# Edge pass of a two-layer graph network: first statistics in the middle of the step, for the group two back; norm rows one step later; a projection between the spreads; powers first on GpSimd

## The chip, the cores and the metric

The kernel runs on one core of one Trainium2 chip, as one program. The metric is the time of the device in microseconds. The kernel before has a median of 2852.71 us over 3 runs (2852.1 to 2857.18).

## The reference, cut to what matters

```
h = maximum(layernorm(x), 0)                       # x: [50000, 128] f32
x = x + HGT(h, node_type (3), edges (25000), edge_type (4))
h = maximum(layernorm(x), 0)
x = x + GraphConv(relu, W2)(GraphConv(relu, W1)(h))

HGT: k, q, v = per-type projections of h; per edge, 8 heads:
  att   = (q[dst] * (k[src] @ rel_att[type])).sum(-1) * rel_pri / sqrt(16)
  alpha = softmax of att over the edges of one dst
  aggr  = segment_sum(alpha * (v[src] @ rel_msg[type]), dst)
  trans = gelu(aggr) @ Wa[type] + ba[type]
  res   = trans * sigmoid(skip) + h * (1 - sigmoid(skip))
  out   = layernorm(res) * ln_g[type] + ln_b[type]
```

The edges are sorted by destination, so a segment sum is a scan along the edges that is reset where the destination changes.

## The kernel before, in words

The kernel runs in phases with barriers between them: tables of the nodes, an attention phase, a softmax over segments (`soft_`), the edge pass (`edge_`, lines 1215 to 1560 of the program), and two graph convolutions (`conv1`, `conv2`). The change lies in the edge pass, beside one allocation at the head.

The edge pass takes 196 tiles of 128 edge places in 28 groups of G = 7 tiles, and each group in two parts (`CK`): 4 tiles (512 columns) and 3 tiles (384). Each engine has a program of its own, written out by hand as a loop over steps s, and semaphores are the only order between them. In before there are 28+3 steps. What a group goes through, with the line of each operation:

- **Spread** (TensorE, L1440, L1443): the softmax weight and the carry factor of each edge are spread over the head's rows into PSUM (`wB`, `dB`), one buffer each.
- **Gather** (VectorE, `gathered`): `msg_all` times `wB` (L1499), then the scan with `dB` (L1503), which carries on from the last column of the part before.
- **Gelu** (ScalarE, L1395) into `gl`, and the **mask product** (GpSimd, L1368), which multiplies `gl` by a mask per node type, `glm`.
- **Projection** (TensorE, `project`): an identity matmul that adds the residual input `hb` (L1453), a bias matmul per tile (L1455), and three matmuls per tile for the types (L1459), all into `pc`, two buffers.
- **First statistics** (VectorE, `spreads(0, ..)`, L1510, L1514, L1518): mean and variance of the projection, plus epsilon. **First power** (GpSimd, L1386): to the power of -1/2. **Scale term** (VectorE, L1528). **Normalisation** (ScalarE, L1407) into `x1`.
- **Gains** (TensorE, L1468, `pg`, one buffer): gain and bias of the layernorm per edge. VectorE multiplies (L1547), adds (L1549), and adds the residual row `xr` (L1551).
- **Second statistics** (VectorE, `spreads(1, ..)`, the same lines), **second power** (GpSimd, L1380), **norm-row terms** (L1535, L1538), **norm rows** (ScalarE, L1420), the store to the table (SyncE, L1344). The residual rows are stored at L1350.
- SyncE loads rows (L1323), one-hot rows (L1327) and masks (L1334) one step ahead. ScalarE prepares `hb` from the rows (L1428).

In step s of before VectorE does: gather(s, first part); scale term(s-2); norm-row terms(s-3); gather(s, second part); gains and residual of s-2, both parts; second statistics(s-2); first statistics(s-1). TensorE: spread(s, 0); gains(s-2, 0); spread(s, 1); project(s-1, 0); gains(s-2, 1); project(s-1, 1). GpSimd: both mask products of s; second power(s-2); first power(s-1). ScalarE: gelu(s, 0); normalisation(s-2); gelu(s, 1); norm rows(s-3); `hb`(s). The names `edge_x`, `edge_sc` and `edge_st` in the profile are `x1`, `sc3` and `st`; `reset` in the profile of this phase is `dhat`.

Of the kernel before, what the change touches and what calls it, by code (L numbers as in the profile page):

```python
# [5 lines left out]
F32 = mybir.dt.float32  # L6
# [7 lines left out]
P = 128  # L14
D = 128
# [48 lines left out]
def hgt_then_graphconv(nc, x, src, dst, edge_type, node_type, Wk, bk, Wq, bq, Wv, bv, Wa, ba, rel_pri, rel_att,  # L64
                       rel_msg, skip, ln_g, ln_b, W1, b1, W2, b2, out):
    top = ExitStack()
    with top, nc.allow_non_contiguous_dma(reason="small parameter and index lists"):
# [55 lines left out]
        rel_k = sb("rel_k", [P, RELS, D], F32)  # L123
        rel_v = sb("rel_v", [P, RELS, D], F32)
# [1148 lines left out]
        with ExitStack() as ctx:  # L1273
# [6 lines left out]
            two, three, four = range(2), range(3), range(4)  # L1280
            xr = [lb(f"xr{b}", [P, G, NW], F32) for b in four]
            mask = [lb(f"mask{k}", [P, 4, TYPES, P], BF16) for k in two]
            oh = [lb(f"oh{b}", [K9, GC], BF16) for b in three]
# [4 lines left out]
            hs = lb("hs", [P, G, D], F32)  # L1288
# [11 lines left out]
            xr_in = [ls(f"xr_in{b}") for b in four]  # L1300
            mask_in = [ls(f"mask_in{b}") for b in two]
            oh_in = [ls(f"oh_in{b}") for b in three]
# [6 lines left out]
            st_done, var1, var2, rstd1, rstd2 = ls("st_done"), ls("var1"), ls("var2"), ls("rstd1"), ls("rstd2")  # L1309
# [7 lines left out]
            with nc.Block() as block:  # L1317
                @block.sync
                def _(sp):
                    def load(g):  # L1320
                        if g >= 4:
                            sp.wait_ge(nm2, g - 3)
                        sp.dma_start(xr[g % 4][:], xd_rows[g * GC:(g + 1) * GC].rearrange("(t p) w -> p t w", p=P)).then_inc(xr_in[g % 4], 16)  # L1323
                        if g >= 3:
                            sp.wait_ge(pg_ready, (g - 2) * 2)
                        for k in range(SPLIT):
                            sp.dma_start(oh[g % 3][k:K9:SPLIT].rearrange("t (n e) -> t n e", e=P),  # L1327
                                         type_row[g * G:(g + 1) * G, TYPES:2 * TYPES].rearrange("n t e -> t n e")).then_inc(oh_in[g % 3], 16)
# [9 lines left out]
                    for s in steps:  # L1338
                        if on(s + 1):
                            load(s + 1)  # L1340
                        g = s - 3
                        if on(g):
                            sp.wait_ge(hs_done, g + 1)
                            sp.dma_start(ta[g * GC:(g + 1) * GC].rearrange("(t p) d -> p t d", p=P), hs[:]).then_inc(hs_out, 16)  # L1344
                        if on(s + 1):
                            load_masks(s + 1)
                        g = s - 2
                        if on(g):
                            sp.wait_ge(x1_done, g + 1)
                            sp.dma_start(x1_rows[g * GC:(g + 1) * GC].rearrange("(t p) d -> p t d", p=P), x1[g % 3][:]).then_inc(x1_out[g % 3], 16)  # L1350
# [5 lines left out]
                def _(pool):  # L1356
# [14 lines left out]
                    for s in steps:  # L1371
                        if on(s):
                            masked(s, 0)
                            masked(s, 1)
                        if on(s - 2):
                            b = (s - 2) % 2
                            pool.wait_ge(var2, s - 1)
                            if s >= 4:
                                pool.wait_ge(nm2, s - 3)
                            pool.tensor_tensor(rstd[1][b][:], ve[1][b][:], mh[:], ALU.pow).then_inc(rstd2, 1)  # L1380
                        if on(s - 1):
                            b = (s - 1) % 2
                            pool.wait_ge(var1, s)
                            if s >= 3:
                                pool.wait_ge(y_done, s - 2)
                            pool.tensor_tensor(rstd[0][b][:], ve[0][b][:], mh[:], ALU.pow).then_inc(rstd1, 1)  # L1386

                @block.scalar
                def _(act):
# [7 lines left out]
                    for s in steps:  # L1397
                        if on(s):
                            gelu(s, 0)
                        g = s - 2  # L1400
# [11 lines left out]
                        if on(s):  # L1412
                            gelu(s, 1)
                        g = s - 3
                        if on(g):
                            act.wait_ge(nm2, g + 1)
                            if g >= 1:
                                act.wait_ge(hs_out, g * 16)
                            for j in range(G):
                                m = nc.scalar.activation(hs[:, j], x1[g % 3][:, j], ACT.Relu, bias=nmr[1][g % 2][:, j:j + 1],  # L1420
                                                         scale=sc3[g % 2][:, j:j + 1])
                            m.then_inc(hs_done, 1)
                        if on(s):
                            act.wait_ge(xr_in[s % 4], s // 4 * 16 + 16)
                            if s >= 2:
                                act.wait_ge(pc_ready, (s - 1) * 2)
                            for j in range(G):
                                nc.scalar.activation(hb[s % 2][:, j], xr[s % 4][:, j, 0:D], ACT.Relu, bias=xr[s % 4][:, j, C_NA:C_NA + 1],  # L1428
                                                     scale=xr[s % 4][:, j, C_RA:C_RA + 1]).then_inc(hb_done, 1)

                @block.tensor
                def _(pe):
# [12 lines left out]
                    def project(g, ck):  # L1445
                        j0, j1 = CK[ck]
                        if ck == 0:
                            pe.wait_ge(oh_in[g % 3], g // 3 * 48 + 48)
# [279 lines left out]
```

## Time and profile before

| | before |
|---|---|
| median of 3 runs | 2852.71 us |
| the profiled execution, device time | 2854.7 us |
| its span, first to last instruction | 2853.0 us |
| mean granted clock of TensorE, whole span | 0.777 |
| busy share: TensorE, VectorE, ScalarE, GpSimd | 65%, 72%, 41%, 58% |
| edge pass, first load to last store issued | 1585.7 to 2077.9 us |

The profile comes from one execution of the program, recorded by the hardware. Times are in us from the start of the span. In a row of the order of time the columns are: start, duration, engine, line, operation, output<-inputs, shapes, count; in brackets the idle time of the engine before it and who ended it. PE is TensorE, PEld its weight loads, DVE VectorE, ACT ScalarE, POOL GpSimd, SP SyncE. PEclk is the granted clock, 1.00 for 2.4 GHz and 0.50 for 1.2 GHz. Where several instructions of one line are merged into one row, the duration is that of them all.

### The profile page before, as it was taken

The numbers are of one execution on the slowest core, as the hardware profiler recorded it, in microseconds if no ns is written. First come the engines' busy times: TensorE is split into PE (matmuls) and PEld (weight loads), VectorE is DVE, ScalarE is ACT, GpSimd is POOL, SyncE is SP. The second block draws the span as 40 slices with busy tenths as digits, with TensorE's granted clock in tenths as the row PEclk, the third lists the DMA queues.
The fourth block names the chain that finished last, engine by engine and source line by source line (L and its number), as shares of the span: only waits on it lengthen the run. The fifth ranks groups of instructions, "written<-read, shape, count | busy, mean of one in ns | idle before, by whom it ended". The sixth has DMA issues, their size and how long they took to land. (4 is left out here: it accounts for less than half of the span.)

```text
span 2853.0 us, 48869 instructions
## 1 busy us (share of the span) xinstructions
PE 1866.8 (65%) x12706; PEld 1449.3 (51%) x12706; DVE 2062.4 (72%) x7060; ACT 1159.7 (41%) x3211; POOL 1655.0 (58%) x1737
## 2 busy tenths in 40 slices
PE   4630001999999999999992677887757763333332
PEld 1100000999999999999992344444435442222221
DVE  7994563999999999999996777777745553333333
ACT  0000001777777777777771345554422221111111
POOL 0002334777777777777761354455467767777776
PEclk9985555999999999999996798899855555555555
DMA  2006774777777777776761344444344442222222
GB/s 52 0 0 202 249 247 134 172 185 184 183 183 184 181 184 185 185 181 184 182 171 33 91 127 123 122 118 124 102 122 132 131 118 72 71 71 70 71 70 52
DMA packets 400270, 374.38 MB, mean 131 GB/s; under 512 B 60254, under 2 KB 342269, under 8 KB 397032
## 3 DMA queue, kind: packets, MB, share of 16 engines
q1 hardware_dynamic: 360856, 276.76, 35.3%
q0 software_dynamic: 31360, 64.76, 10.7%
q10 hardware_dynamic: 7806, 29.98, 2.6%
q8 instruction: 104, 1.70, 0.2%
q14 instruction: 144, 1.18, 0.2%
HBM read 227.43 MB, written 147.13 MB: 131 GB/s over the span
## 5 line engine op out<-in xcount | busy, mean ns | idle before, releaser
L1683 DVE TENSOR_TENSOR_SCAN conv_sT<-keep,conv_sT,conv_pT 128x128 f32<-128x128 bf16 x390 | 187.1, 480 | 384.3 <-PE conv_pT L1658 383.5
L1658 PE MATMUL conv_pT<-ident,conv_row 128*128 128x128 f32 x392 | 182.1, 464 | 405.2 <-ACT conv_row L1643 328.3
L814 POOL DMA_INDIRECT att_xsd<-xt,ends_i x392 | 390.2, 995 | 95.1 <-issue 94.7
L1658 PEld LDWEIGHTS conv_pT<-ident,conv_row 128*128 128x128 f32 x392 | 74.5, 190 | 496.2 <-ACT conv_row L1643 384.9
L995 PE MATMUL att_kvc<-att_hm,w_kv 128*128 128x128 f32 x2352 | 295.9, 276 | 0.0
L939 ACT ACTIVATE att_nhb<-att_nxr 128x128 f32<-128x128 f32 x391 | 168.8, 478 | 276.6 <-DMA att_nxr<-xt 276.6
L995 PEld LDWEIGHTS att_kvc<-att_hm,w_kv 128*128 128x128 f32 x2352 | 279.6, 193 | 0.0
L1368 POOL TENSOR_TENSOR edge_glm<-edge_gl,edge_mask 128x1536 f32<-128x1536 f32 (+1 forms) x56 | 153.1, 2735 | 214.2 <-PE edge_pc L1459 207.4
L1664 PE MATMUL conv_pm<-w,conv_sT 128*128 128x128 f32 x784 | 258.9, 434 | 12.1 <-DVE conv_res L1690 11.0
L1643 ACT ACTIVATE conv_row<-conv_row,ats 128x128 f32<-128x128 f32 x196 | 78.6, 401 | 425.3 <-DMA conv_row<-t,idx 425.3
L1108 DVE TENSOR_TENSOR att_kvm<-att_kvc,att_rel_in 128x1024 f32<-128x1024 f32 x196 | 240.0, 1224 | 13.1 <-PE att_kvc L1008 1.2
L1008 PE MATMUL att_kvc<-tab,att_noh 9*128 9x128 bf16 x391 | 53.4, 216 | 279.7 <-DMA att_noh<-node_hot 276.7
L1606 POOL DMA_INDIRECT conv_row<-t,idx x196 | 192.0, 979 | 69.4 <-issue 38.4
L1612 POOL DMA_INDIRECT out_dram<-conv_res,out_i x196 | 197.3, 1006 | 59.7 <-issue 58.5
L1606 POOL DMA_INDIRECT conv_row<-ta,idx x196 | 185.1, 944 | 68.2 <-issue 52.4
L1664 PEld LDWEIGHTS conv_pm<-w,conv_sT 128*128 128x128 f32 x784 | 205.9, 323 | 32.5 <-DVE conv_sT L1683 29.0
L1044 PE MATMUL att_keyp<-att_kvm,rel_k 128*128 128x128 f32 x1568 | 207.4, 275 | 0.5 <-DVE att_prod L1140 0.5
L1046 PE MATMUL att_msgp<-att_kvm,rel_v 128*128 128x128 f32 x1568 | 207.1, 275 | 0.0
L1044 PEld LDWEIGHTS att_keyp<-att_kvm,rel_k 128*128 128x128 f32 x1568 | 190.5, 192 | 4.4 <-issue 0.9
L1046 PEld LDWEIGHTS att_msgp<-att_kvm,rel_v 128*128 128x128 f32 x1568 | 190.8, 192 | 0.0
L829 POOL TENSOR_TENSOR att_not<-att_nx,rb_all 128x256 f32<-128x256 f32 x196 | 142.5, 727 | 82.1 <-DMA out_dram<-att_not 50.9
L1151 DVE TENSOR_TENSOR att_hm<-att_hT,att_mask_in_t 128x768 f32<-128x768 f32 x196 | 186.2, 950 | 3.2 <-DMA att_mask_in_t<-type_row 3.2
(240 smaller groups left out, 4883.6 us busy)
## 6 DMA issues: line engine op xcount, KB each, us to landing
att_mask_in_t<-type_row SPq DMA_DIRECT2D x196, 192.0 KB
xt<-xr ACTq DMA_DIRECT2D x23, 1224.0 KB
att_nxr<-xt SPq DMA_DIRECT2D x97, 262.0 KB
att_rel_in<-rel_row SPq DMA_DIRECT2D x196, 128.0 KB, 3.2
out_dram<-att_not SPq DMA_DIRECT2D x97, 256.0 KB, 3.8
ta<-att_nhs SPq DMA_DIRECT2D x97, 256.0 KB
xr<-in_x_dram SPq DMA_DIRECT2D x22, 1088.0 KB
xd_rows<-att_xsd SPq DMA_DIRECT2D x196, 65.5 KB, 3.1
```

What stands on the lines that cost most here:

```text
L814: pool.indirect_dma_start(out=xsd[:, v, k, :], out_offset=None, in_=xt, in_offset=bass.IndirectOffsetOnAxis(ap=ends_i[:, n, k:k + 1], axis ...
L939: m = nc.scalar.activation(nhb[:, u % 2, i], nxr[g % RN][:, j, 0:D], ACT.Relu, bias=nxr[g % RN][:, j, C_NA:C_NA + 1], scale=nxr[g % RN][:, ...
L995: nc.tensor.matmul(kvc[:, e], w_kv[:, t, e], hm[:, w, 0, t], start=e == 0 and t == 0, stop=False)
L1044: nc.tensor.matmul(keyp[:, 0], rel_k[:, r], kvm[:, w, 0, r], start=r == 0, stop=r == RELS - 1)
L1046: m = nc.tensor.matmul(msgp[:, 0], rel_v[:, r], kvm[:, w, 1, r], start=r == 0, stop=r == RELS - 1)
L1108: dve.tensor_tensor(kvm[:, w], kvc[:, 0:2].rearrange("p a (o e) -> p a o e", o=1).to_broadcast([P, 2, RELS, P]), rel_in[:, v].rearrange("p ...
L1151: dve.tensor_tensor(hm[:, w], hT[:, 0:2].rearrange("p e (o d) -> p e o d", o=1).to_broadcast([P, 2, TYPES, P]), mask_in_t[:, k % RM], ALU. ...
L1606: pool.indirect_dma_start(out=row[:, n % R, :], out_offset=None, in_=table, in_offset=bass.IndirectOffsetOnAxis(ap=idx[:, int(second), n:n ...
L1612: pool.indirect_dma_start(out=out, out_offset=bass.IndirectOffsetOnAxis(ap=out_i[:, k:k + 1], axis=0), in_=res[:, k % R, :], in_offset=Non ...
L1658: nc.tensor.transpose(pT[:, n % 2, 0:P], row[:, n % R], ident[:]).then_inc(t_ready, 1)
L1664: nc.tensor.matmul(pm[:, k % 2, 0:D], sT[:, k % R], w[:], start=True, stop=True).then_inc(m_ready, 1)
L1683: dve.tensor_tensor_scan(sT[:, n % R], keep[:, n * P:(n + 1) * P], pT[:, n % 2, 0:P], before, ALU.mult, ALU.add).then_inc(s_ready, 1)
```

## The change

VectorE's step becomes: gains and residual (s-3, first part); gather(s, first part); norm-row terms(s-4); first statistics(s-2); gains(s-3, second part); gather(s, second part); scale term(s-2); residual(s-3, second part); second statistics(s-3). TensorE: spread(s, 0); gains(s-3, 1); project(s-1, 0); spread(s, 1); project(s-1, 1); gains(s-2, 0). GpSimd: first power(s-2), both mask products of s, second power(s-3). ScalarE: `hb`(s); gelu(s, 0); norm rows(s-4); gelu(s, 1); normalisation(s-2). There are 28+4 steps. The rows get a fifth buffer, the one-hot rows a fourth, and `hs` takes the place of the relation tables, which are no longer read in this phase. The semaphore of the statistics is split in two.

```diff
-        rel_k = sb("rel_k", [P, RELS, D], F32)
-        rel_v = sb("rel_v", [P, RELS, D], F32)
+        rel_kv = sb("rel_kv", [P, 2, RELS, D], F32)
+        rel_k, rel_v = rel_kv[:, 0], rel_kv[:, 1]
...
-            hs = lb("hs", [P, G, D], F32)
+            hs = rel_kv[:].rearrange("p a r d -> p (a r) d")[:, 0:G]
-            steps = range(groups + 3)
+            steps = range(groups + 4)
 # sync
+                        if g >= 5:
+                            sp.wait_ge(nm2, g - 4)
+                        sp.dma_start(xr[g % 5][:], ...
                         if g >= 4:
-                            sp.wait_ge(nm2, g - 3)
-                        sp.dma_start(xr[g % 4][:], ...
-                        if g >= 3:
-                            sp.wait_ge(pg_ready, (g - 2) * 2)
+                            sp.wait_ge(pg_ready, (g - 3) * 2)
...
                         g = s - 3
                         if on(g):
+                            sp.wait_ge(x1_done, g + 1)
+                            sp.dma_start(x1_rows[...], x1[g % 3][:]).then_inc(x1_out[g % 3], 16)
+                        if on(s + 1):
+                            load_masks(s + 1)
+                        g = s - 4
+                        if on(g):
                             sp.wait_ge(hs_done, g + 1)
                             sp.dma_start(ta[...], hs[:]).then_inc(hs_out, 16)
-                        if on(s + 1):
-                            load_masks(s + 1)
-                        g = s - 2
-                        if on(g):
-                            sp.wait_ge(x1_done, g + 1)
-                            sp.dma_start(x1_rows[...], x1[g % 3][:]).then_inc(x1_out[g % 3], 16)
 # gpsimd
+                        g = s - 2
+                        if on(g):
+                            b = g % 2
+                            pool.wait_ge(var1, g + 1)
+                            if g >= 2:
+                                pool.wait_ge(y_done, g - 1)
+                            pool.tensor_tensor(rstd[0][b][:], ve[0][b][:], mh[:], ALU.pow).then_inc(rstd1, 1)
                         if on(s):
                             masked(s, 0)
                             masked(s, 1)
-                        if on(s - 2):            # second power, then first power(s - 1)
...
+                        g = s - 3                # second power
...
 # scalar: hb(s), gelu(s, 0), norm rows (s - 4), gelu(s, 1), normalisation (s - 2)
 # tensor
                         if on(s):
                             spread(s, 0)
-                        if on(s - 2):
-                            gains(s - 2, 0)
+                        if on(s - 3):
+                            gains(s - 3, 1)
+                        if on(s - 1):
+                            project(s - 1, 0)
                         if on(s):
                             spread(s, 1)
                         if on(s - 1):
-                            project(s - 1, 0)
+                            project(s - 1, 1)
                         if on(s - 2):
-                            gains(s - 2, 1)
-                        if on(s - 1):
-                            project(s - 1, 1)
+                            gains(s - 2, 0)
 # vector
+                    def gained(g, ck):           # multiply and add, as before
...
+                    def residual(g, ck):
+                        js = slice(*CK[ck])
+                        dve.wait_ge(pg_read, g * 2 + ck + 1)
+                        m = dve.tensor_tensor(x1[g % 3][:, js], x1[g % 3][:, js], xr[g % 5][:, js, 0:D], ALU.add)
+                        if ck:
+                            m.then_inc(x1_done, 1)
                     for s in steps:
+                        g = s - 3
+                        if on(g):
+                            gained(g, 0)
+                            residual(g, 0)
                         if on(s):
                             gathered(s, 0)
+                        g = s - 4                # norm-row terms, wait for rstd2
...
+                        g = s - 2
+                        if on(g):
+                            spreads(0, g, pc[g % 2], var1)
+                        g = s - 3
+                        if on(g):
+                            gained(g, 1)
+                        if on(s):
+                            gathered(s, 1)
                         g = s - 2
                         if on(g):
                             dve.wait_ge(rstd1, g + 1)
                             dve.scalar_tensor_tensor(nmr[0][g % 2][:], ...).then_inc(nm1, 1)
                         g = s - 3
                         if on(g):
+                            residual(g, 1)
                             dve.wait_ge(x1_done, g + 1)
-                            stats[0] += 1
-                            spreads(1, g, x1[g % 3], stats[0], var2)
-                        g = s - 1
-                        if on(g):
-                            stats[0] += 1
-                            spreads(0, g, pc[g % 2], stats[0], var1)
+                            spreads(1, g, x1[g % 3], var2)
```

## Rows read from the trace of the kernel before

**Rows 1.** The windows view: busy time of each engine in 100 us of the pass.
```profile
core 0: us, PE busy (x) PEld busy (x) DVE busy (x) ACT busy (x) POOL busy (x), PEclk, DMA share, GB/s
1800.00:1900.00 100.00, 78.60 (x407) 47.61 (x405) 78.81 (x256) 50.69 (x133) 50.55 (x24) 0.91 0.44 124
```

**Rows 2.** Order of time: VectorE's first gather product, fourth and last full step.
```profile
1624.42 0.69 DVE L1499 TENSOR_TENSOR msg_all<-edge_wB,msg_all 128x512 f32<-128x512 f32 x1
...
2034.40 0.69 DVE L1499 TENSOR_TENSOR msg_all<-edge_wB,msg_all 128x512 f32<-128x512 f32 x1
```

**Rows 3.** Order of time: one steady step, VectorE, TensorE and GpSimd.
```profile
1915.66 1.28 DVE L1503 TENSOR_TENSOR_SCAN msg_all<-edge_dB,msg_all 128x512 f32<-128x512 f32 x1
...
1918.43 1.92 PE L1453 MATMUL edge_pc<-edge_hb,ident 128*128 128x512 f32 x2
...
1918.75 1.02 DVE L1503 TENSOR_TENSOR_SCAN msg_all<-edge_dB,msg_all 128x384 f32<-128x384 f32 x1 [1.00 <-PE edge_dB L1443]
1919.68 0.66 DVE L1547 TENSOR_TENSOR edge_x<-edge_x,edge_pg 128x512 f32<-128x512 f32 x1
...
1920.63 2.94 PE L1459 MATMUL edge_pc<-w_a,edge_glm 128*128 128x128 f32 x24
...
1923.75 3.10 POOL L1368 TENSOR_TENSOR edge_glm<-edge_gl,edge_mask 128x1536 f32<-128x1536 f32 x1 [7.17 <-PE edge_pc L1459]
...
1924.11 0.56 DVE L1547 TENSOR_TENSOR edge_x<-edge_x,edge_pg 128x384 f32<-128x384 f32 x1 [2.32 <-PE edge_pg L1468]
...
1925.05 2.27 PE L1459 MATMUL edge_pc<-w_a,edge_glm 128*128 128x128 f32 x18
1925.29 1.98 DVE L1551 TENSOR_TENSOR edge_x<-edge_x,edge_xr 128x384 f32<-128x384 f32 x1
...
1927.49 2.37 POOL L1368 TENSOR_TENSOR edge_glm<-edge_gl,edge_mask 128x1152 f32<-128x1152 f32 x1 [0.64 <-PE edge_pc L1459]
...
1928.02 1.02 PE L1443 MATMUL edge_dB<-reset,expand 112*128 112x512 f32 x2
...
1929.40 0.49 DVE L1518 TENSOR_SCALAR edge_ve<-edge_mv 128x7 f32<-128x7 f32 x1
1929.80 1.47 DVE L1510 BATCH_NORM_STATS2 edge_st<-edge_pc 128x6 f32<-128x128 f32 x7
...
1931.92 0.17 DVE L1518 TENSOR_SCALAR edge_ve<-edge_mv 128x7 f32<-128x7 f32 x1
```

**Rows 4.** Order of time, end of the pass: residual addition alone; the last norm rows.
```profile
2058.13 0.56 DVE L1551 TENSOR_TENSOR edge_x<-edge_x,edge_xr 128x384 f32<-128x384 f32 x1
...
2075.03 2.80 ACT L1420 ACTIVATE edge_hs<-edge_x,edge_nmr,edge_sc 128x128 f32<-128x128 f32 x7 [4.74 <-DVE edge_nmr L1538]
```

**Rows 5.** Order of time, attention phase: VectorE with two SBUF operands beside GpSimd.
```profile
1193.77 0.72 POOL L829 TENSOR_TENSOR att_not<-att_nx,rb_all 128x256 f32<-128x256 f32 x1 [1.61 <-DMA out_dram<-att_not]
1193.81 0.70 DVE L1090 SCALAR_TENSOR_TENSOR att_nnm<-att_nmv,att_nrs 128x4 f32<-128x4 f32 x1
...
516.71 1.25 DVE L1090 SCALAR_TENSOR_TENSOR att_nnm<-att_nmv,att_nrs 128x4 f32<-128x4 f32 x1
517.05 0.19 POOL L821 COPY ats<-att_xsd 128x6 f32<-128x6 f32 x1
517.21 0.72 POOL L829 TENSOR_TENSOR att_not<-att_nx,rb_all 128x256 f32<-128x256 f32 x1
```

**Rows 6.** Order of time, attention phase: a sum of two SBUF operands during a power.
```profile
492.34 1.68 POOL L848 TENSOR_TENSOR att_nrs<-att_nve,att_mh 128x8 f32<-128x8 f32 x1
...
493.06 0.42 DVE L1143 TENSOR_TENSOR att_nx<-att_nx,att_nxr 128x256 f32<-128x256 f32 x1
```

**Rows 7.** Order of time, start of the pass: the very first projection, at full clock.
```profile
1597.57 1.02 PE L1453 MATMUL edge_pc<-edge_hb,ident 128*128 128x512 f32 x2
...
1598.85 2.94 PE L1459 MATMUL edge_pc<-w_a,edge_glm 128*128 128x128 f32 x24
```

**Rows 8.** The windows view of TensorE alone: a steady step, and early in the pass.
```profile
1918.60:1920.40 1.80, 1.80 (x5) 0.51 0.87 240
...
1610.60:1612.40 1.80, 1.80 (x3) 0.50 0.90 268
```

More of the change, by code:

```diff
@@ L1279, in hgt_then_graphconv @@
             CK = ((0, 4), (4, G))
-            two, three, four = range(2), range(3), range(4)
-            xr = [lb(f"xr{b}", [P, G, NW], F32) for b in four]
+            two, three, four, five = range(2), range(3), range(4), range(5)
+            xr = [lb(f"xr{b}", [P, G, NW], F32) for b in five]
             mask = [lb(f"mask{k}", [P, 4, TYPES, P], BF16) for k in two]
-            oh = [lb(f"oh{b}", [K9, GC], BF16) for b in three]
+            oh = [lb(f"oh{b}", [K9, GC], BF16) for b in four]
             gl = lb("gl", [P, GC], F32)
@@ L1299, in hgt_then_graphconv @@
             pg = lp("pg", [P, 4, GW], F32)
-            xr_in = [ls(f"xr_in{b}") for b in four]
+            xr_in = [ls(f"xr_in{b}") for b in five]
             mask_in = [ls(f"mask_in{b}") for b in two]
-            oh_in = [ls(f"oh_in{b}") for b in three]
+            oh_in = [ls(f"oh_in{b}") for b in four]
             x1_out = [ls(f"x1_out{b}") for b in three]
@@ L1398, in _ @@
                         if on(s):
-                            gelu(s, 0)
+                            act.wait_ge(xr_in[s % 5], s // 5 * 16 + 16)
+                            if s >= 2:
+                                act.wait_ge(pc_ready, (s - 1) * 2)
+                            for j in range(G):
+                                nc.scalar.activation(hb[s % 2][:, j], xr[s % 5][:, j, 0:D], ACT.Relu, bias=xr[s % 5][:, j, C_NA:C_NA + 1],
+                                                     scale=xr[s % 5][:, j, C_RA:C_RA + 1]).then_inc(hb_done, 1)
+                            gelu(s, 0)
+                        g = s - 4
+                        if on(g):
+                            act.wait_ge(nm2, g + 1)
+                            if g >= 1:
+                                act.wait_ge(hs_out, g * 16)
+                            for j in range(G):
+                                m = nc.scalar.activation(hs[:, j], x1[g % 3][:, j], ACT.Relu, bias=nmr[1][g % 2][:, j:j + 1],
+                                                         scale=sc3[g % 2][:, j:j + 1])
+                            m.then_inc(hs_done, 1)
+                        if on(s):
+                            gelu(s, 1)
                         g = s - 2
@@ L1467, in gains @@
                         for j in range(j0, j1):
-                            m = nc.tensor.matmul(pg[:, j - j0], oh[g % 3][:, j * P:(j + 1) * P], tab9[:, CW:CW + GW], start=True, stop=True)
+                            m = nc.tensor.matmul(pg[:, j - j0], oh[g % 4][:, j * P:(j + 1) * P], tab9[:, CW:CW + GW], start=True, stop=True)
                         m.then_inc(pg_ready, 1)
@@ L1504, in gathered, with spreads @@
                                                ALU.mult, ALU.add).then_inc(scan_done, 1)
-                    def spreads(k, g, of, done, then):
+                    def spreads(k, g, of, then):
+                        measured = st1_done if k else st0_done
                         for j in range(G):
@@ L1510, in spreads @@
                             m = dve.bn_stats(st[:, k, j], of[:, j])
[L1511 to L1512 removed]
+                        m.then_inc(measured, 1)
+                        dve.wait_ge(measured, g + 1)
                         for j in range(G):
```

93 lines of the change are left out of this document (32 added, 61 removed).

## The prediction

> **What bounds the kernel now.** I read the page first, then the windows of the edge pass, then one step of it in order of time, because shares of a span cannot say which wait ends last. In the windows VectorE and TensorE are each busy 79% of the stretch and GpSimd half [rows 1]: nobody is full, so the step is a loop of waits. It repeats exactly: 24 periods from 1624.42 to 2034.40 are 17.08 us each [rows 2].
>
> The loop [rows 3]: the first scan ends at 1916.94. TensorE then does the second spread and the first projection of the group before, to 1920.63+2.94 = 1923.57. Only then can GpSimd's first mask product start (1923.75 to 1926.85), and only then the gain matmuls for which VectorE had waited 2.32 us. VectorE's last residual addition starts at 1925.29 and takes 1.98 us, where the same one takes 0.56 us with GpSimd idle [rows 4]; it ends just after the mask product. The second projection ends at 1925.05+2.27 = 1927.32, the second mask product runs from 1927.49 to 1929.86, and the 7-element addition of epsilon that falls into it takes 0.49 us instead of 0.17 and ends with it. The first statistics (1929.80 to 1932.09) and the next step follow. VectorE so loses 1.0 (second scan) + 2.3 (gains) + 1.4 (residual) + 0.3 (epsilon) = 5.0 us a step; 12.1 us is its work.
>
> **What blocks VectorE beside GpSimd.** This decides the forecast. An operation of VectorE with two SBUF operands stands still while a GpSimd product runs: one of 4 elements, 0.15 us alone, took 0.70 us from 1193.81, beside a product that ended at 1194.49 [rows 5]. At 516.71 one took 1.25 us, through two GpSimd operations that stood back to back [rows 5], so the seam between two such does not let VectorE in. A product with a PSUM operand is not touched (0.56 us at 1924.11, inside the first mask product) [rows 3]. The power is another thing: a sum of two SBUF operands took its usual 0.42 us in the middle of one [rows 6], so a power blocks nothing.
> The Trainium skill (SBUF — State Buffer, Who interferes with whom) says that a VectorE instruction with two SBUF inputs contends with any GpSimd instruction that reads SBUF. The power reads SBUF, and the row speaks against the rule there. By the page the first residual addition would wait about 0.15 us a step for the second power, 4 us in all; by the row nothing.
>
> **The change, part by part.** One new steady step on VectorE, 0 being the start of its first gain product, durations from [rows 3] unless said:
> - Gains and residual of the first four tiles of the group three back: three operations of 0.7 us, to 2.1. Their inputs come from the step before. The wait of 2.3 us goes here.
> - Gather, first part: product 0.7, scan 1.28, to 4.05. Two small norm-row operations, to 4.35; the power they need came at the end of the step before.
> - First statistics: 1.47+0.6+0.17, to 6.55. Their projection is a step old and GpSimd is idle, so nothing blocks.
> - Gains of the last three tiles: two operations of 0.56, to 7.7. Gather, second part: product to 8.2, then scan 1.02 once its spread is there, to 9.3.
> - GpSimd: the first power stands ahead of the masks, 6.6 to 8.1 (1.48, an estimate from the 1.68 of 8 elements [rows 6]); then the first mask product, 8.1 to 11.2.
> - VectorE's scale term and last residual addition both read two SBUF operands. They come up at 9.3 and are blocked until 11.2: a new stall of 1.9 us in place of the old ones.
> - Second statistics: 2.1, with an epsilon at their end that the second mask product can block.
>
> TensorE with the clock at 2.4 GHz: gain matmuls at 1.4, after the second gain operation, the identity matmul some 0.4 later; from identity to the end of the 24 matmuls took 1598.85+2.94-1597.57 = 4.2 us [rows 7], so the first projection ends at 6.1. The spread of 512 took 1927.32 to 1929.04, 1.7 us; that of 384, at three quarters, 1.3, ends at 7.4. Second projection 3.4, to 10.8. The next gains and spread end at 13.2. The second scan finds its spread ready: TensorE leaves VectorE's loop, and the wait of 1.0 goes.
>
> The second mask product (2.37 us) needs that projection plus 0.17, and so it decides the period:
> *Long step.* Ready at 11.0, it stands behind the first (end 11.2) without a seam, to 13.6, and VectorE is let in only then: scale term 0.15, residual 0.56, statistics 2.1. Period 16.4.
> *Short step.* With the projection 0.3 us or more late VectorE slips in at 11.2; scale term and residual are done at 11.9, aggregation at 14.0, and the epsilon ends with the second product. With a lateness x the period is 10.8+x+0.17+2.37+0.17 = 13.5+x, and not under about 14.3.
> The clock sets x. Now it is at 1.2 GHz for part of each step after 3.2 us of idle, and early in the pass it was so after 1.4 us of idle too [rows 8]; the identity then takes 1.92 us [rows 3] instead of 1.02 [rows 7]. In a long step TensorE idles from 13.2 to 17.8, in a short one some 2 us. So I expect a slow stretch in most steps: gain matmuls +0.3 and rest +0.2 (estimates), identity +0.9, x = 1.4, period 14.9. With one long step in four, (3x14.9+16.4)/4 = 15.3, which I take. Ends for a steady step: 14.4 and 16.5.
>
> Covered, at nothing: ScalarE has 50.7 us of work in 100 [rows 1], 8.7 a step; its normalisation starts after the scale term at 11.4, is half done by 12.9 and done by 14.0, before VectorE's next step wants it. Late by a us there would be a us per step. SyncE: the input load waits for the norm terms at 4.35 and is wanted by ScalarE some 10 us later; the masks stand behind the store of the residual rows, issued at 12, and are wanted at 8.1 of the next step, 11 us later; the table store goes out near 15 and its buffer is wanted 5 us later. DMA is 44% busy [rows 1], and no wait in [rows 3] is for a transfer. The powers stay two. The fifth input buffer, fourth one-hot buffer and shared place of the norm rows issue nothing.
>
> Start and end. From [rows 7] the very first projection ends at 1601.8; then spread 1.5, projection 3.4, spread 1.8, projection 4.3, spread 1.5, projection 3.4, gains 0.6: the fourth step starts at 1618.3 and its gather at 1620.4, against 1624.4 now [rows 2], 4 us earlier. The last full step starts 24 periods on. From there: one period; 10.3 for a step that TensorE's last projections bound; 8.9 and 6.2 for two of VectorE alone; 4.8 for power, terms and norm rows. The end is at 1618.3+25P+30.2 = 1648.5+25P, with P = 15.3 at 2031.0. Now it is 2075.03+2.80 = 2077.8 [rows 4]: 46.8 us gained. The added step of the tail is in this: from the last full step's gather the rest takes 43.4 us now and 43.5 then.
>
> The profiled execution took 2854.7 us (span 2853.0, 1.7 around it), 2.0 over the median 2852.7. 2854.7-46.8 = 2807.9, in terms of the median 2806.
>
> **Rivals.**
> 1. *Long steps throughout.* P = 16.4: end 2058.5, gain 19, time 2833. For it: the back-to-back rows, and a margin of 0.2 us only. Against: TensorE would idle 4.6 us in such a step, and 3.2 already brings the low clock. Chance 0.19.
> 2. *Hardly any block.* The scale term finds a way in, or less is locked than I read: VectorE's 12.1 and TensorE's 12 us decide, P = 13, gain 104, time 2748; half-way (14.2) 2778. For it: powers block nothing. Against: the 1.98 us row and the two of [rows 5]. Chance 0.10.
> 3. *Slower: the low clock takes hold of the projection.* P passes 17.07 when the second projection is 3.6 us late, which needs 7.2 of its 9.4 us at 1.2 GHz. At 17.8 the time is 2868, with all of it slow (P about 20) 2924. For it: the low clock comes after short idles too. Against: TensorE would be busy from 1.4 to 13.2 with no wait. Chance 0.06.
> 4. *It does not do what it says:* masks, queued behind the residual store, or input rows arrive late and take 1.7 us a step back. P = 17.0, 2848. For it: shorter leads. Against: DMA at 44%. Chance 0.05.
> The forecast has 0.60, with 2788 to 2821 (P 14.6 to 15.9) by itself.
>
> **How the numbers follow.** A measurement here tells about 0.2%, 6 us, from nothing. Faster: forecast, rivals 1 and 2, 0.89, of which I keep 0.87. Within: most of rival 4, 0.05. Slower: rival 3 and what could ride on it, 0.08. The range goes from P = 14.4 (gain 69) to a little past the long step: 2783 to 2839.
>
> **What would show it.** Right: steps of 15 to 16 us; a scale term of about 2 us that ends with the first mask product; no wait of the last gain product or second scan for TensorE; first statistics while GpSimd idles; the last epsilon ending with the second mask product. Wrong: scale terms of 0.14 us (rival 2), of 4 us in every step (rival 1), a granted clock under 0.8 in the pass (rival 3), GpSimd or ScalarE waiting for a DMA (rival 4).

## The result and the profile after

The changed kernel takes 2786.8 us (median of 4 runs, 2786.3 to 2789.5). Its ratio to the kernel before is 0.977, with a 95% interval of 0.975 to 0.978: 66 us less. (One of the four executions of the kernel before took 3608 us and is left out.) The forecast was 2806 in a range of 2783 to 2839, so the direction and the range hold, but the gain is two fifths larger than the 47 us worked out.

| | before | after |
|---|---|---|
| span of the profiled execution | 2853.0 | 2784.7 us |
| start of the last norm rows | 2075.0 | 2005.8 us |
| mean of the 24 steady periods | 17.08 | 14.375 us |

All of it came from the edge pass: the last norm rows end 69.2 us earlier. The page, first section (engine, busy time and its share of the span, instructions): the same instructions as before.
```profile
PE 1840.5 (66%) x12706; PEld 1453.7 (52%) x12706; DVE 2059.3 (74%) x7060; ACT 1168.4 (42%) x3211; POOL 1660.8 (60%) x1737
```
The windows of the pass, in the columns of [rows 1], which answers to it. VectorE is busy 92 of 100 us instead of 79. The granted clock is the same in this stretch; over the 24 steady periods it is 0.94, against 0.90 before.
```profile
1800.00:1900.00 100.00, 86.64 (x462) 57.64 (x461) 91.83 (x300) 63.78 (x161) 59.22 (x29) 0.91 0.56 147
...
1616.50:1961.50 345.00, 300.38 (x1635) 198.59 (x1633) 321.14 (x1030) 218.36 (x549) 206.35 (x96) 0.94 0.54 143
```
The steps are not alike. Measured from one first gain product of VectorE to the next, 14 of the 24 are 13.6 to 13.9 us long, seven 14.65 to 14.74 and three 16.1 to 16.3. Here are rows of a short one in order of time; it starts at 1630.10 and the next at 1643.94. It answers to [rows 3].
```profile
1636.45 0.17 DVE L1520 TENSOR_SCALAR edge_ve<-edge_mv 128x7 f32<-128x7 f32 x1
1636.70 1.48 POOL L1378 TENSOR_TENSOR edge_rstd<-edge_ve,edge_mh 128x7 f32<-128x7 f32 x1 [4.95 <-DVE edge_ve L1520]
1638.15 5.81 POOL L1368 TENSOR_TENSOR edge_glm<-edge_gl,edge_mask 128x1536 f32<-128x1536 f32 x2
1638.46 2.27 PE L1460 MATMUL edge_pc<-w_a,edge_glm 128*128 128x128 f32 x18
1639.11 2.16 DVE L1567 SCALAR_TENSOR_TENSOR edge_nmr<-edge_mv,edge_rstd 128x7 f32<-128x7 f32 x1
1641.19 0.54 DVE L1534 TENSOR_TENSOR edge_x<-edge_x,edge_xr 128x384 f32<-128x384 f32 x1
1641.77 1.45 DVE L1512 BATCH_NORM_STATS2 edge_st<-edge_x 128x6 f32<-128x128 f32 x7
1643.86 0.17 DVE L1520 TENSOR_SCALAR edge_ve<-edge_mv 128x7 f32<-128x7 f32 x1
1643.94 0.69 DVE L1527 TENSOR_TENSOR edge_x<-edge_x,edge_pg 128x512 f32<-128x512 f32 x1
```
Two things are to be seen. The scale term of 7 elements takes 2.16 us and ends with the first mask product: this is the stall the forecast put there. And the residual addition behind it, which reads two SBUF operands, runs at 1641.19 although the two mask products stand back to back (one row of 5.81 us, where 3.10+2.37 is 5.47). VectorE was let in at the seam (the moment between the two products), and GpSimd waited for it. With the view cut at the seam, another such step shows the second product at 2.77 us against its usual 2.37, beside the same addition.
```profile
1627.34 0.54 DVE L1534 TENSOR_TENSOR edge_x<-edge_x,edge_xr 128x384 f32<-128x384 f32 x1
...
1627.35 2.77 POOL L1368 TENSOR_TENSOR edge_glm<-edge_gl,edge_mask 128x1152 f32<-128x1152 f32 x1
```
A step of 16.2 us, in order of time, starts at 1875.23 and ends at 1891.46:
```profile
1879.98 4.58 PE L1460 MATMUL edge_pc<-w_a,edge_glm 128*128 128x128 f32 x24
...
1885.25 0.56 DVE L1500 TENSOR_TENSOR msg_all<-edge_wB,msg_all 128x384 f32<-128x384 f32 x1 [2.44 <-PE edge_wB L1441]
...
1886.70 2.27 PE L1460 MATMUL edge_pc<-w_a,edge_glm 128*128 128x128 f32 x18
1886.89 0.96 DVE L1567 SCALAR_TENSOR_TENSOR edge_nmr<-edge_mv,edge_rstd 128x7 f32<-128x7 f32 x1
1889.15 2.37 POOL L1368 TENSOR_TENSOR edge_glm<-edge_gl,edge_mask 128x1152 f32<-128x1152 f32 x1 [1.31 <-PE edge_pc L1460]
1890.46 1.08 DVE L1520 TENSOR_SCALAR edge_ve<-edge_mv 128x7 f32<-128x7 f32 x1
1891.46 0.67 DVE L1527 TENSOR_TENSOR edge_x<-edge_x,edge_pg 128x512 f32<-128x512 f32 x1
```
Here the first projection's 24 matmuls take 4.58 instead of 2.94 us, the second projection ends late, at 1888.97, the second mask product starts behind it at 1889.15, and the epsilon is held until it ends at 1891.52. There is a new wait too: the second gather product stands 2.44 us for its spread, which the change put behind the first projection. The windows of TensorE over a step of 13.86, one of 16.29 and one of 14.66 us (columns: stretch, length, TensorE busy, granted clock, DMA share, GB/s) show what parts them:
```profile
1643.94:1657.80 13.86, 11.62 (x68) 1.00 0.60 154
1701.03:1717.32 16.29, 14.79 (x68) 0.79 0.53 142
1717.32:1731.98 14.66, 13.19 (x68) 0.88 0.51 140
```

### The profile page after: what moved, and what is told of

Its sections match the earlier page's. It is cut to its first block and busy times, and to the rows that moved or that the text cites. A ratio compares the mean times of both kernels' runs of the same rounds, so it can differ in the third digit from the quotient of the medians.

```text
span 2784.7 us, 48869 instructions
## 1 busy us (share of the span) xinstructions
PE 1840.5 (66%) x12706; PEld 1453.7 (52%) x12706; DVE 2059.3 (74%) x7060; ACT 1168.4 (42%) x3211; POOL 1660.8 (60%) x1737
## 5 line engine op out<-in xcount | busy, mean ns | idle before, releaser
L1044 PE MATMUL att_keyp<-att_kvm,rel_kv 128*128 128x128 f32 x1568 | 207.4, 275 | 0.5 <-DVE att_prod L1140 0.5
L1046 PE MATMUL att_msgp<-att_kvm,rel_kv 128*128 128x128 f32 x1568 | 207.1, 275 | 0.0
L1044 PEld LDWEIGHTS att_keyp<-att_kvm,rel_kv 128*128 128x128 f32 x1568 | 190.5, 192 | 4.4 <-issue 0.9
L1046 PEld LDWEIGHTS att_msgp<-att_kvm,rel_kv 128*128 128x128 f32 x1568 | 190.8, 192 | 0.0
L1063 DVE BATCH_NORM_STATS2 att_nst<-att_nx 128x6 f32<-128x128 f32 x782 | 186.3, 279 | 0.2
```

What stands on the lines that cost most here:

```text
L1044: nc.tensor.matmul(keyp[:, 0], rel_k[:, r], kvm[:, w, 0, r], start=r == 0, stop=r == RELS - 1)
L1046: m = nc.tensor.matmul(msgp[:, 0], rel_v[:, r], kvm[:, w, 1, r], start=r == 0, stop=r == RELS - 1)
L1063: m = dve.bn_stats(nst[:, k, i], of[:, u % 2 * 2 + i])
```

## The experiments

They ran in three rounds, each with the kernel before beside it; the changed kernel itself ran beside them only in the second. On the chips of the first and third round that kernel took 2957 and 2970 us, on the second 2851. In the profiles the time behind the edge pass is the longer one there (from the last norm rows to the end 867 us in the first kernel below, 776 in the changed kernel's own profile), while a step at full clock takes the same 13.85 us (two added matmuls, below). So the rounds are compared by ratios and by steps. A step is always measured between VectorE's gain products of 512 columns, and a mean is over the 24 periods from the fourth step on.

**TensorE's order undone.** The second spread goes ahead of the first projection again. The gain matmuls stay where the change put them.
```diff
                             gains(s - 3, 1)
+                        if on(s):
+                            spread(s, 1)
                         if on(s - 1):
                             project(s - 1, 0)
-                        if on(s):
-                            spread(s, 1)
-                        if on(s - 1):
                             project(s - 1, 1)
```


> One part undone: TensorE does the second spread before the first projection again, as in the kernel before; all else as changed. Theory A (the projection must end early enough for GpSimd's second mask product): the second spread waits for the first scan at 4.05 of the step, so the projections end about 1.3 us later; period 14.9 at full clock, 15.6 in the mean against 14.4, so about 2816 us and mask products that start after the projection, not after the power. Rival B (TensorE is off the loop, its order is of no account): 2787 within 6 us.

Ratio 0.9715 (0.9697 to 0.9732), steps of 13.2 to 13.3 and 15 us after a first one of 16.4, mean 13.86. Both theories fell: undoing this part makes the kernel faster than the change as a whole. A step of 13.3 us, in order of time from 1804.57, and the start of the next:
```profile
1813.12 1.02 DVE L1503 TENSOR_TENSOR_SCAN msg_all<-edge_dB,msg_all 128x384 f32<-128x384 f32 x1
1814.06 0.14 DVE L1566 SCALAR_TENSOR_TENSOR edge_nmr<-edge_mv,edge_rstd 128x7 f32<-128x7 f32 x1
1814.11 0.55 DVE L1533 TENSOR_TENSOR edge_x<-edge_x,edge_xr 128x384 f32<-128x384 f32 x1
1814.30 5.66 POOL L1368 TENSOR_TENSOR edge_glm<-edge_gl,edge_mask 128x1536 f32<-128x1536 f32 x2 [1.17 <-PE edge_pc L1460]
1816.80 0.85 DVE L1519 TENSOR_SCALAR edge_ve<-edge_mv 128x7 f32<-128x7 f32 x1
...
1819.34 1.17 DVE L1533 TENSOR_TENSOR edge_x<-edge_x,edge_xr 128x512 f32<-128x512 f32 x1
1819.93 1.92 POOL L1388 TENSOR_TENSOR edge_rstd<-edge_ve,edge_mh 128x7 f32<-128x7 f32 x1
```
The projection is later, as expected, and that holds the first mask product back until 9.7 us into the step, where it began 8.1 us into the one above. By then the scale term (0.14 us) and the residual have gone ahead of it. What is blocked now is the epsilon (0.85 instead of 0.17 us) and 0.5 us of the first residual. The later mask product was a gain here, because it missed VectorE's scale term and last residual.

**Powers last on GpSimd.** The block of the first power is moved behind `masked(s, 1)`.
```diff
+                        if on(s):
+                            masked(s, 0)
+                            masked(s, 1)
                         g = s - 2            # first power
...
-                        if on(s):
-                            masked(s, 0)
-                            masked(s, 1)
```


> One part undone: GpSimd does both mask products first, then the first power (two back), then the second power (three back). Theory A: the first power then waits for the second mask product (ends about 13.4 of the step), VectorE stands at the scale term until 14.9; period about 17.7 against 14.4, 24 x 3.3 = 80 us, about 2867. Rival B (a power of 1.5 us can stand anywhere in an engine that is 60% busy): 2787 to 2800.

Ratio 1.029 (1.028 to 1.031), slower than before, steps of 20.49 us. The mechanism is there: VectorE stands 6.01 us at the scale term for the power that ends behind the second mask product.
```profile
1865.23 2.37 POOL L1368 TENSOR_TENSOR edge_glm<-edge_gl,edge_mask 128x1152 f32<-128x1152 f32 x1 [1.31 <-PE edge_pc L1460]
1867.55 1.48 POOL L1381 TENSOR_TENSOR edge_rstd<-edge_ve,edge_mh 128x7 f32<-128x7 f32 x1
1869.07 0.17 DVE L1567 SCALAR_TENSOR_TENSOR edge_nmr<-edge_mv,edge_rstd 128x7 f32<-128x7 f32 x1 [6.01 <-POOL edge_rstd L1381]
...
1876.66 4.46 PE L1460 MATMUL edge_pc<-w_a,edge_glm 128*128 128x128 f32 x24
```
The step is 2.8 us longer than the 17.7 worked out, because the clock is at 1.2 GHz for part of every step (granted 0.75 over the pass): the 24 projection matmuls take 4.46 instead of 2.94 us and the identity 2.08 instead of 1.02. So the place of the power ahead of the masks carries the change: without it nothing is gained.

**Two more matmuls a step.**
```diff
+                        if ck == 0 and g >= 3:
+                            nc.tensor.matmul(wB[:, 0:w], expand[:, blk], what[:, at:at + w], start=True, stop=True)
+                            nc.tensor.matmul(wB[:, 0:w], expand[:, blk], what[:, at:at + w], start=True, stop=True)
                         nc.tensor.matmul(wB[:, 0:w], ...).then_inc(w_ready, 1)
```


> Two more wB matmuls of 512 columns per step (same operands, same target, before the one that counts), 1.7 us of TensorE, from the fourth step on, where TensorE idles waiting for VectorE. Theory A (steps of 14.7 and 16.2 us are those in which TensorE's clock was at 1.2 GHz after an idle; at full clock a step is 13.85): nearly all steps 13.85, 24 x 0.5 = 12 us less, about 2775, although TensorE does more. Rival B (the long steps come from something else, such as a transfer or the mask products): 2787 or up to 10 us more, steps of 14.7 and 16.2 stay.

Ratio 0.9738 (0.9717 to 0.9760), and every step but the first is 13.84 to 13.86 us, mean 13.88. Theory A holds: with the clock at full (1.00 below, in the columns of [rows 1]) there is no step of 14.7 or 16.2. The gain on the change, 9 us by the ratios, is a little under the 12 expected.
```profile
1800.00:1900.00 100.00, 96.38 (x515) 60.58 (x515) 97.26 (x317) 66.58 (x168) 64.27 (x30) 1.00 0.57 150
```

**Last residual early.** `residual(g, 1)` moves from behind the scale term to right behind `gained(g, 1)`.
```diff
                             gained(g, 1)
+                            residual(g, 1)
...
-                            residual(g, 1)
                             dve.wait_ge(x1_done, g + 1)
```


> The residual addition of the last three tiles moves from behind the scale term to right behind its gains, where GpSimd runs only a power. Theory A (the scale term alone waits for the first mask product, the 0.55 us of the residual behind it is on the path): full-clock steps 13.3 instead of 13.85, low-clock ones as now; 24 x 0.35 = 8 us less, about 2779. Rival B (the addition, which reads two SBUF operands, now holds GpSimd's mask product up by as much): 2787.

Ratio 0.9777 (0.9761 to 0.9793): no gain over the change. The steps run 13.4, 16.3, 14.7 in turn, mean 14.78. The full-clock step is 13.4, as theory A has it, but only a third of the steps are of that kind. In the others the clock was low (granted 0.88 over the pass), and that took the gain back. Rival B is out as well, since the 13.4 is there.

**The changed kernel again,** on the chip of this round.

> The changed kernel as it is, on the chip of the other kernels of this round, so that they can be set against it. Steps of 13.85, 14.7 and 16.2 us, mean 14.4; ratio to the kernel before 0.977.

Ratio 0.977 (0.975 to 0.979), mean step 14.32.

**First statistics behind the second gather.**
```diff
                         g = s - 3
                         if on(g):
                             gained(g, 1)
                         if on(s):
                             gathered(s, 1)
+                        g = s - 2
+                        if on(g):
+                            spreads(0, g, pc[g % 2], var1)
```


> One part moved: the first statistics (two back) stand behind the second gather instead of ahead of the last gains. Theory A (the power, and the mask products queued behind it, wait for these statistics): power to 12.2 of the step, first mask product from 12.2, which catches the scale term: blocked to 15.3, then residual and statistics: steps of 18.2 us, 24 x 3.8 = 91 us more than as changed, slower than before. Rival B (only their being two groups back matters, not the place in the step): steps of 14.4.

Ratio 1.033 (1.031 to 1.034), steps of 20.5 us, slower than before. The sequence is theory A's, power, mask products and then a scale term caught for their first:
```profile
1879.28 1.48 POOL L1378 TENSOR_TENSOR edge_rstd<-edge_ve,edge_mh 128x7 f32<-128x7 f32 x1 [11.59 <-DVE edge_ve L1520]
1880.72 3.09 POOL L1368 TENSOR_TENSOR edge_glm<-edge_gl,edge_mask 128x1536 f32<-128x1536 f32 x1
1880.79 3.05 DVE L1567 SCALAR_TENSOR_TENSOR edge_nmr<-edge_mv,edge_rstd 128x7 f32<-128x7 f32 x1 [1.59 <-POOL edge_rstd L1378]
```
The 2.3 us over the 18.2 expected are again with a clock at 1.2 GHz for part of each step. That the statistics are two groups back is not enough; behind the second gather they hold up the power and the mask products.

**TensorE's order undone, first gather ahead of the first residual.** The edit on TensorE is the one shown above.
```diff
                             gained(g, 0)
-                            residual(g, 0)
                         if on(s):
                             gathered(s, 0)
+                        if on(g):
+                            residual(g, 0)
```


> TensorE's order as before the change (it gave steps of 13.3) and VectorE's first gather ahead of the first residual addition. Theory A (in those steps the loop is: gains, second gather product's spread after the first scan, projection, first mask product, epsilon at the seam): the scan comes 1.0 us earlier, steps of 12.3 to 12.5 at full clock, so 24 us less than with TensorE's order alone, some 36 under the changed kernel. Rival B (VectorE's own work and blocks bound the step, and an order inside it gives nothing): 13.3.

Ratio 0.973 (0.971 to 0.975), mean 14.01. Every second step is 14.33 us, those between are 13.0 to 13.8 with two of 14.6 and 15.1. Wrong for both. In every second step the mask product starts just ahead of the scale term (1761.63 against 1761.99), which then takes 2.77 us; in the next one the scale term is 0.5 us ahead (1776.32 against 1776.86) and takes 0.14. Bringing the chain forward by 1 us brought the mask product into VectorE's way again.
```profile
1761.63 5.82 POOL L1368 TENSOR_TENSOR edge_glm<-edge_gl,edge_mask 128x1536 f32<-128x1536 f32 x2 [0.57 <-PE edge_pc L1460]
1761.99 2.77 DVE L1567 SCALAR_TENSOR_TENSOR edge_nmr<-edge_mv,edge_rstd 128x7 f32<-128x7 f32 x1
...
1776.32 0.14 DVE L1567 SCALAR_TENSOR_TENSOR edge_nmr<-edge_mv,edge_rstd 128x7 f32<-128x7 f32 x1
1776.86 5.50 POOL L1368 TENSOR_TENSOR edge_glm<-edge_gl,edge_mask 128x1536 f32<-128x1536 f32 x2 [1.47 <-PE edge_pc L1460]
```

**The same with epsilon on GpSimd.** The addition of epsilon goes from the end of `spreads` to GpSimd, ahead of each power.
```diff
-                        dve.tensor_scalar_add(ve[k][g % 2][:], mv[k][g % 2][:, :, 1], EPS).then_inc(then, 1)
...
+                            pool.tensor_scalar(ve[0][b][:], mv[0][b][:, :, 1], EPS, None, ALU.add).then_inc(eps_done, 1)
... (the same for the second power, with its wait; TensorE's order and the first gather as above)
```


> As the one with TensorE's order and gather first, and epsilon added by GpSimd ahead of each power instead of by VectorE. Theory A (once the scan is early TensorE's own chain of 12.4 bounds, the block of the epsilon is beside the path): within 0.3 us of the step without this edit, 12.3 to 12.5. Rival B (the epsilon at the seam is what ends the step): a further 0.5 to 1.5 us a step less, 12 to 36 us.

Ratio 0.970 (0.968 to 0.971), median 2764.2 against 2773.5 without the edit on the same chip, so 9 us, less than rival B's least and more than theory A's most. The profiled execution, at 2773.9 us, was ten above the other three (2763.3 to 2764.5), and its mean step of 14.05 can't be set against the 14.01 of the kernel without the edit. What the epsilon is worth alone stays between the two theories.

**The kernel before with more matmuls.**
```diff
+                        if ck == 0 and g >= 3:
+                            for _ in range(3):
+                                nc.tensor.matmul(dB[:, 0:w], expand[:, blk], dhat[:, at:at + w], start=True, stop=True)
                         nc.tensor.matmul(dB[:, 0:w], ...).then_inc(d_ready, 1)
```


> The kernel BEFORE the change, with three more dB matmuls of 512 columns per step (same operands and target, ahead of the one that counts), 2.6 us of TensorE where it idled 3.2 us. Theory A (in the kernel before the 1.2 GHz stretch lies on the loop: second spread +0.8, identity +0.9 us): steps of 15.4 to 15.6 instead of 17.07, 25 x 1.5 = 38 us less, ratio 0.987; so more than half of what the change brought could be had by keeping the clock. Rival B (the added work delays the spread, or the slow stretch is hidden): ratio 1.00 or above.

Ratio 0.996 (0.993 to 0.998), between the two theories. The ten runs fall in two groups, six of 2945 to 2954 us and four of 2967 to 2972, against 2970 for the kernel before. In the profiled one, the slowest of all, the steps go 15.8 and 18.3 in turn, with two of 17.0, mean 17.07. So it settles less than it should. The clock lies on the loop of the kernel before: in the short steps, where it is mostly up (granted 0.94), the wait for the second spread is 0.27 us instead of 1.00 and that for the gains 1.33 instead of 2.32. But these matmuls did not keep it up: it stayed at 0.91, although TensorE was busy 94 of 100 us, and in a long step the 24 matmuls took 4.68 us. Why the clock fell here and not with the two matmuls above is open. An estimate from the steps near full clock: 15.8 in the old order and 13.85 in the changed one, so about 1.9 of the 2.7 us a step are the order's and not the clock's.
```profile
1797.96 4.68 PE L1462 MATMUL edge_pc<-w_a,edge_glm 128*128 128x128 f32 x24
1815.16 2.94 PE L1462 MATMUL edge_pc<-w_a,edge_glm 128*128 128x128 f32 x24
...
1818.64 0.56 DVE L1550 TENSOR_TENSOR edge_x<-edge_x,edge_pg 128x384 f32<-128x384 f32 x1 [1.33 <-PE edge_pg L1471]
...
1800.00:1900.00 100.00, 94.02 (x435) 56.57 (x434) 79.18 (x257) 50.73 (x133) 50.62 (x24) 0.91 0.45 126
```

**Scale term and residual ahead of the masks, epsilon on GpSimd.** TensorE's order is the changed one. The edit of epsilon is the one above.
```diff
                             gained(g, 1)
+                            residual(g, 1)
+                        g = s - 2
+                        if on(g):
+                            dve.wait_ge(rstd1, g + 1)
+                            dve.scalar_tensor_tensor(nmr[0][g % 2][:], ...).then_inc(nm1, 1)
                         if on(s):
                             gathered(s, 1)
...
                         if on(s):
+                            if on(s - 2):
+                                pool.wait_ge(nm1, s - 1)
                             masked(s, 0)
```


> The changed kernel, TensorE's order as changed; the scale term and the last residual addition stand right behind the last gains and ahead of the second gather, GpSimd's mask products wait for the scale term, and GpSimd adds epsilon. So no operation of VectorE with two SBUF operands is left beside a mask product but the first residual addition. Theory A (the block of 1.9 us on the scale term is what the changed step has too much): steps of 12.5 to 12.9 at full clock, 13.3 in the mean, ratio about 0.968. Rival B (TensorE's new order or the clock bounds the step): 13.8 to 14.4, ratio 0.974 to 0.977.

Ratio 0.9593 (0.9565 to 0.9621), steps of 12.36 us, alike but for one pair of 12.8 and 11.95, clock 1.00. Theory A's cause holds and rival B is out; the gain is larger than theory A said (12.5 at full clock, 13.3 in the mean, ratio 0.968), mostly because no step had the clock low. The scale term takes 0.17 us, and the wait added to GpSimd costs 0.28:
```profile
1884.71 0.17 DVE L1572 SCALAR_TENSOR_TENSOR edge_nmr<-edge_mv,edge_rstd 128x7 f32<-128x7 f32 x1 [0.33 <-POOL edge_rstd L1382]
1884.95 5.44 POOL L1369 TENSOR_TENSOR edge_glm<-edge_gl,edge_mask 128x1536 f32<-128x1536 f32 x2 [0.28 <-DVE edge_nmr L1572]
```

**All together:** these edits, the second spread ahead of the first projection as before the change, and the first gather ahead of the first residual.

> The same edits with TensorE's order as before the change and the first gather ahead of the first residual addition. Theory A (blocks off the path, TensorE's chain of spread, two projections and gains bounds): 12.5 at full clock, 13.0 in the mean, ratio about 0.961. Rival B (the store of the norm rows, for whose buffer ScalarE already waits 2.6 us a step, or the low clock bounds): 14.1, ratio 0.970.

Ratio 0.9559 (0.9538 to 0.9581), steps of 12.13 us, the fastest of all, and faster than both kernels. Theory A (12.5 at full clock, ratio 0.961) is nearer than rival B (14.1), and again the gain is larger than it said. TensorE is now at 98% and its clock at 1.00; ScalarE waits about 3 us a step for the store of its norm rows, and no step came near rival B's 14.1.
```profile
1800.00:1900.00 100.00, 97.58 (x564) 62.93 (x564) 92.03 (x343) 75.16 (x194) 74.61 (x50) 1.00 0.60 170
```

## Why the prediction was right, point by point

*Right: the loop opens at VectorE's waits.* VectorE no longer waits for the last gain matmuls (one wait of 3.4 us in 380 us instead of 2.32 in each step) nor for the second spread's carry factor (1.6 us in all). The first statistics run while GpSimd idles (4.95 us idle before the power).

*Right: the block of the scale term.* Forecast 1.9 us until the first mask product ends; rows of 2.16 us measured in the full-clock steps, with its own 0.14 in them. The experiment that takes it, the last residual and the epsilon out of the way of the masks brings the step to 12.36; the residual alone brought 0.45 of these 1.5 us at full clock (13.4).

*Right: a power blocks nothing.* The first residual addition took its usual 0.69 us although it began 0.2 us before a power's end (1892.89, the power from 1891.62 to 1893.10). A fuller case stands in the kernel with scale term and residual ahead of the masks (last two rows below): the last residual addition took its usual 0.56 us wholly inside a power. The Trainium skill (SBUF — State Buffer, Who interferes with whom) says that a VectorE instruction with two SBUF inputs contends with a GpSimd instruction that reads SBUF. By that rule both would have waited, and these rows speak against it. The reverse exists: a power that came up behind a held addition took 1.92 instead of 1.48 us (1819.93, above).
```profile
1891.62 1.48 POOL L1388 TENSOR_TENSOR edge_rstd<-edge_ve,edge_mh 128x7 f32<-128x7 f32 x1
1892.89 0.69 DVE L1534 TENSOR_TENSOR edge_x<-edge_x,edge_xr 128x512 f32<-128x512 f32 x1
...
1883.18 1.50 POOL L1382 TENSOR_TENSOR edge_rstd<-edge_ve,edge_mh 128x7 f32<-128x7 f32 x1
1883.82 0.56 DVE L1540 TENSOR_TENSOR edge_x<-edge_x,edge_xr 128x384 f32<-128x384 f32 x1
```

*Wrong: the seam.* The prediction said of two products back to back that VectorE "is let in only then", behind the second, and so gave the full clock a long step of 16.4 us. Measured, VectorE gets in at every such seam (all 14 full-clock steps) and the second product waits 0.4 us. At full clock the step is 13.85 us, the shortest there is, not the longest; rival 1 had its sign turned round. [Rows 5] had led there: at 516.71 the small term did outlast two GpSimd operations. What differs there was not tested: the first of the two is a copy of 0.19 us, and the term came up before the copy, while GpSimd was still on an indirect transfer (516.10 to 517.04).

*Wrong in size: how often the clock is low.* "A slow stretch in most steps", each 14.9: in fact ten of 24, seven of 14.7 and three of 16.2, mean 15.1. The rule that the lateness of the second projection is added to the step is borne out: it ends 10.6 us into a step of 13.84, 12.2 into one of 14.66 and 13.7 into one of 16.23. But for the last two the rule gives 0.2 us too much, and its floor of 14.3 was 0.45 too high. What decides when the clock falls is open. The steps from 1630.10 and 1687.19 are alike (TensorE 11.62 us busy, granted 1.00), and the one is followed by a step at 1.00, the other by one at 0.79. The "1.4 us of idle" of the prediction are two pauses, of 0.95 and 0.41 us; counted the same way its 3.2 are 3.6. Together: 14 x 13.83 + 7 x 14.69 + 3 x 16.2 = 345, over 24 = 14.375, where I had 15.3. These are the 22 us of the pass's gain that the forecast lacked (24 x 0.93).

*Not seen: the price of "a projection between the spreads".* I costed it as harmless, since TensorE leaves VectorE's loop. It brought a wait of its own for the second spread in low-clock steps (13.3 us in ten waits over 380 us), and undone it saves 0.5 us a step: 13.86 against 14.32 to 14.375, on another chip. Of the parts tried, the places of the first statistics and of the first power are both needed for any gain, and this one costs. That the gains moved a step later was not tried alone.

*Start and end:* the fourth step started at 1616.5 (forecast 1618.3); from the start of the last full step to the end it took 2008.6-1961.5 = 47.1 us (45.5 with a longer period in it). The tail is 3 us longer than worked out. The steady step of 14.375 is in fact a hair below the forecast's own lower end of 14.4, and it is this longer tail that kept the time 4 us inside the range. That the range holds is narrow, and in part luck.

Rivals 3 and 4 did not come: the granted clock did not fall (0.94 against 0.90), and in the 24 steady periods nothing but ScalarE's norm rows, up to 2.2 us, waited for a transfer. The chance given to rival 2 included a half-way case of 2778, which the result came near to, by another way: not by fewer blocks, but by the seam.

## What to carry to other kernels

Where VectorE and GpSimd share a step, draw up which of VectorE's operations read two SBUF operands (and the small `tensor_scalar` after statistics), and place them in GpSimd's gaps by a wait: 0.3 us of waiting on GpSimd took 1.5 us out of the step (with the last residual and the epsilon moved too) and made nearly all steps alike. Test each part of a reordering alone, since one of three here was a loss hidden in a gain. And read the step in each of its kinds: a mean of 14.4 was three different steps, set apart by the granted clock.

## What the runs showed of the hardware that I had not expected

- VectorE's waiting operation is let in at the seam of two GpSimd mask products that follow each other without a gap, and the second then takes 2.77 instead of 2.37 us.
- The low clock came with TensorE 94% busy (0.91 granted, kernel before with added matmuls), and stayed away at 94% (steps of 12.36) and 96% (added matmuls after the change). Busy share alone does not tell; a matmul at the low clock is also busy for longer (24 matmuls 4.68 against 2.94 us).
- A longer step can lengthen itself: where an order cost more than 3 us a step (powers last, statistics late), the granted clock was 0.75 and 0.83 and the step grew by 2 to 3 us more than worked out.
